# Attention and fp8 layer on one core: both score pairs ahead of the weighing in quads with a fix, side products in two parts

## The reference, cut to what matters

```
h = layernorm(x)                       # no learned scale
q, k, v = h @ Wq, h @ Wk, h @ Wv
latent = (k + v) @ W_down              # 32 wide; k_rec = latent @ W_up_k, v_rec = latent @ W_up_v
scores = clip(q k_rec^T * scale) * decay(|i - j|)
x = x + softmax(clip(scores)) @ v_rec (heads joined) @ Wo
x = x + fp8_gemm(layernorm(x) in bf16, kernel) + bias
```

## Time and profile before

| | |
|---|---|
| median of 3 runs | 525.74 us |
| profiled execution | 525.57 us |
| its span | 523.8 us |
| TensorE, ScalarE, VectorE, GpSimd busy | 93%, 94%, 53%, 42% |
| mean granted TensorE clock | 0.989 |
| first and last exponential start | 14.0, 502.0 us |

### The profile page before, as it was taken

One profiled execution on the slowest core, in us unless ns is written; L12 is line 12 of the kernel. 1 busy time (PEld: TensorE's weight loads), 2 busy tenths in 40 slices (PEclk: granted clock), 3 DMA queues, 4 the chain that ended last, 5 costly groups with the idle time before them and its releaser, 6 DMA issues.

```text
span 523.8 us, 9403 instructions
## 1 busy us (share of the span) xinstructions
PE 486.4 (93%) x3452; PEld 111.6 (21%) x3452; DVE 277.5 (53%) x646; ACT 490.0 (94%) x535; POOL 219.2 (42%) x285
## 2 busy tenths in 40 slices
PE   8899999999999999999999999999999999999961
PEld 3311211122122212122121212122121212121220
DVE  6515554555654564546645564554654564445646
ACT  4789999999999999999999999999999999999961
POOL 0989429790720249971450229992101121002110
PEclk9999999999999999999999999999999999999995
DMA  6689889947994104567966002747977000100000
GB/s 178 200 244 222 312 201 219 335 181 167 248 211 106 29 7 162 203 243 158 256 161 139 8 5 76 272 167 203 262 159 183 8 4 7 48 0 2 1 21 24
DMA packets 50483, 73.79 MB, mean 141 GB/s; under 512 B 6208, under 2 KB 29184, under 8 KB 50432
## 3 DMA queue, kind: packets, MB, share of 16 engines
q1 hardware_dynamic: 49344, 72.72, 50.6%
q10 hardware_dynamic: 1088, 0.41, 0.3%
HBM read 35.40 MB, written 35.65 MB: 136 GB/s over the span
## 4 chain that ended last, share of the span: by engine, by line
PE 56%; ACT 29%; issue 7%; DVE 7%; DVEq 0%; ACTq 0%
ACT probs L770 29%; PE ps L970 27%; PE ps L954 16%; DVE ps L1206 3%; PE ps L834 2%; PE ps L950 2%; PE ps L839 1%; PE ps L867 1%; PE ps L830 1%; PE ps L862 1%; PE ps L809 1%; PE ps L824 0%; PE ps L874 0%; DVE xn L1254 0%; PE ps L880 0%
## 5 line engine op out<-in xcount | busy, mean ns | idle before, releaser
L770 ACT ACTIVATE probs<-ps 128x1024 f32<-128x1024 f32 x512 | 478.9, 1061 | 9.5 <-DVE ps L1206 5.9
L970 PE MATMUL ps<-probs,V 128*9 128x512 f32 x2048 | 267.8, 594 | 3.2 <-ACT probs L770 0.8
L1206 DVE TENSOR_TENSOR ps<-ps,consts 128x256 f32<-128x256 f32 (+1 forms) x256 | 144.3, 566 | 173.3 <-PE ps L954 166.0
L954 PE MATMUL ps<-Qs,Ks 64*128 64x512 bf16 x992 | 179.0, 385 | 13.6 <-ACT probs L770 6.9
L954 PEld LDWEIGHTS ps<-Qs,Ks 64*128 64x128 bf16 x992 | 42.7, 93 | 281.0 <-ACT probs L770 266.5
L970 PEld LDWEIGHTS ps<-probs,V 128*9 128x9 f32 x2048 | 31.3, 88 | 80.5 <-issue 59.8
L572 POOL TENSOR_SCALAR rs<-mv 128x4 f32<-128x4 f32 (+1 forms) x10 | 2.3, 231 | 102.7 <-DVEq L1388 102.2
L1214 DVE COPY pv_out<-ps 105x512 f32<-105x512 f32 x31 | 21.4, 692 | 34.4 <-PE ps L970 34.4
L655 POOL TENSOR_TENSOR xs<-xs,magic 128x512 f32<-128x512 f32 x7 | 8.9, 1278 | 70.3 <-DVE magic L1267 70.3
L606 POOL TENSOR_TENSOR sq<-sq,parts 128x1024 f32<-128x1024 f32 (+1 forms) x16 | 28.4, 1773 | 1.3
L608 POOL TENSOR_TENSOR parts<-sq,parts 128x1024 bf16<-128x1024 f32 (+1 forms) x16 | 28.3, 1771 | 1.3
(11 more groups left out here) (148 smaller groups left out, 280.9 us busy)
## 6 DMA issues: line engine op xcount, KB each, us to landing
Qs<-qp_dram SPq DMA_DIRECT2D x26, 512.0 KB, 8.7
qp_dram<-parts SPq DMA_DIRECT2D x14, 768.0 KB, 5.2
Ks<-kp_dram SPq DMA_DIRECT2D x26, 384.0 KB, 5.7
kp_dram<-parts SPq DMA_DIRECT2D x12, 384.0 KB, 3.4
kp_dram<-parts SPq DMA_DIRECT2D x6, 768.0 KB, 4.4
qp_dram<-parts SPq DMA_DIRECT2D x7, 512.0 KB, 6.3
Qs<-qp_dram SPq DMA_DIRECT2D x10, 256.0 KB, 9.4
X<-L_attn_x SPq DMA_DIRECT2D x9, 256.0 KB, 3.1
```

The costliest lines, as they stand in the source:

```text
L770: nc.scalar.activation(probs[:, quad % RING, 2 * jp:2 * jp + 2, :].rearrange("p j n -> p (j n)"), ps_all[:, bank * CH:(bank + 2) * CH], AC ...
L954: last = nc.tensor.matmul(bank, Ks[half, g, jp, key_cols(v, kc)], Qs[half, g, jp, qh, v, :], start=True, stop=True)
L970: last = nc.tensor.matmul(pv[32 * j:32 * j + VW, :], V[:, unit // 2 * NB + kc, HG * j + g, :], probs[:, quad % RING, j, :], start=i == 0, ...
L1206: nc.vector.tensor_tensor(own, own, factors, ALU.mult).then_inc(fixed, 1)
```

## The change

Four things change. (a) In a quad with a fix (not in the fp32 group) TensorE makes the scores of both slots before it weighs quad - 2, and a side product of that quad lies between the two. (b) The products sp, proj, k, q, v and n (from quad 13 of the program on) are made in two parts, the first two quads ahead of the second; only the second signals, only the first waits. (c) Quads of products move: for batch 1 second keys 28 to 30, first queries 30 to 34; for the later batches first queries 28 to 30 and second queries 38 to 34; the tail's xqT and y of odd units' rows from 30 and 34 to 36 and 38; in the last unit the turns from 12, 18, 26 to 18, 22, 26. (d) VectorE's reciprocals go from quad 7 to quad 6, and GpSimd makes late keys before a result.

```diff
-TAIL_ROWS = [28 if not is_shared(_u) else 34 if _u % 2 else 30 for _u in range(UNITS)]
-TAIL_PRODUCTS = [30 if not is_shared(_u) else 36 if _u % 2 else 34 for _u in range(UNITS)]
+TAIL_ROWS = [(34 if _u % 2 else 36) if is_shared(_u) else 28 for _u in range(UNITS)]
+TAIL_PRODUCTS = [(36 if _u % 2 else 38) if is_shared(_u) else 30 for _u in range(UNITS)]
...
-        (6 if _b else 14, "T", 0), (18, "T", 1), (22 if _b else 26, "k", 0), (26 if _b else 28, "k", 1),
-        (28 if _b else 30, "q", 0), (38, "q", 1), (50, "v", 0), (54, "v", 1))]
+        (6 if _b else 14, "T", 0), (18, "T", 1), (22 if _b else 26, "k", 0), (26 if _b else 30, "k", 1),
+        (30 if _b else 34, "q", 0), (34 if _b else 38, "q", 1), (50, "v", 0), (54, "v", 1))]
...
-JOBS += [((UNITS - 1) * UNIT_QUADS + _q, "turn", _g) for _g, _q in enumerate((12, 18, 26))]
+JOBS += [((UNITS - 1) * UNIT_QUADS + _q, "turn", _g) for _g, _q in enumerate((18, 22, 26))]
...
-PE_SIDE = {_q: (_k, _i) for _q, _k, _i in JOBS}
+PARTED = [_j for _j in JOBS if _j[0] > NB + 4 and _j[1] in ("sp", "proj", "k", "q", "v", "n")]
+PE_SIDE = {_q: (_k, _i, 1 if (_q, _k, _i) in PARTED else None) for _q, _k, _i in JOBS}
+PE_SIDE.update({_q - 2: (_k, _i, 0) for _q, _k, _i in PARTED})
...
                 if b < B - 1:
                     early_parts(b + 1)
+                    late_keys(b + 1)
                     if b > 0:
                         result(2 * b - 1)
-                    late_keys(b + 1)
...
-            def spread_sums(unit, bank):
-                pe.wait_ge(spread, unit + 1)
-                nc.tensor.matmul(bank, same_head, wide[:, :], start=True, stop=True).then_inc(spread_ps, 1)
+            def spread_sums(unit, bank, part=None):
+                if part != 1:
+                    pe.wait_ge(spread, unit + 1)
+                cols = slice(0, CH) if part is None else half_cols[part]
+                last = nc.tensor.matmul(bank[:, cols], same_head, wide[:, cols], start=True, stop=True)
+                if part != 0:
+                    last.then_inc(spread_ps, 1)
...
+            def head_norms(b, bank, part=None):
+                if part != 1:
+                    pe.wait_ge(sq_ready, b + 1)
+                for a in range(2) if part is None else (part,):
...
+                both_first = not in_f32 and variant(quad)[1] is not None
...
                     qk(s)
-                    if quad >= 2 and s % 2 == in_f32:
+                    if s % 2 == 0 and quad in PE_SIDE and both_first:
+                        job(*PE_SIDE[quad])
+                    if quad >= 2 and s % 2 == (in_f32 or both_first):
                         weigh(quad - 2)
-                if quad in PE_SIDE:
+                if quad in PE_SIDE and not both_first:
...
-                if at == 7:
+                if at == 6:
                     invert_sums(unit)
                     widen_sums(unit)
```

More of the change, by code:

```diff
@@ L141 @@
 JOB_ORDER = [(_k, _i) for _, _k, _i in JOBS] + [(_k, UNITS + _n) for _n in range(LOOPED_UNITS) for _k in ("proj", "xqT", "y")]
-PE_SIDE = {_q: (_k, _i) for _q, _k, _i in JOBS}
+PARTED = [_j for _j in JOBS if _j[0] > NB + 4 and _j[1] in ("sp", "proj", "k", "q", "v", "n")]
+PE_SIDE = {_q: (_k, _i, 1 if (_q, _k, _i) in PARTED else None) for _q, _k, _i in JOBS}
+PE_SIDE.update({_q - 2: (_k, _i, 0) for _q, _k, _i in PARTED})
+assert len(PE_SIDE) == len(JOBS) + len(PARTED)
 DVE_SIDE = {_q + (_q > FIRST_VALUES): (_k, _i) for _q, _k, _i in JOBS}
@@ L825, in transpose_x, with columns, own_rows, project_k @@
                 last.then_inc(tr_ps, 1)
[L827 to L837, removed]
+            pairs = (range(0, 2), range(2, 4))
+            def columns(bank, part):
+                return bank if part is None else bank[:, half_cols[part]]
+            def own_rows(n, part):
+                first = n % 2 * CH + (0 if part is None else part * HALF)
+                return slice(first, first + (CH if part is None else HALF))
+            def project_k(n, bank, part=None):
+                if part != 1:
+                    pe.wait_ge(xnT_ready, n + 1)
+                last = nc.tensor.matmul(columns(bank, part), wk_eff[:, :], xnT[:, own_rows(n, part)], start=True, stop=True)
+                if part != 0:
+                    last.then_inc(k_ps, 1)
+            def project_q(n, bank, part=None):
+                last = nc.tensor.matmul(columns(bank, part), wq_s[:, :], xnT[:, own_rows(n, part)], start=True, stop=True)
+                if part != 0:
+                    last.then_inc(q_ps, 1)
+            def project_v(n, bank, part=None):
+                for t in range(4) if part is None else pairs[part]:
                     at = n % 2 * CH + t * P
@@ L840, in project_v @@
                                             start=True, stop=True)
[L841 to L845, removed]
+                if part != 0:
+                    last.then_inc(v_ps, 1)
+            def head_norms(b, bank, part=None):
+                if part != 1:
+                    pe.wait_ge(sq_ready, b + 1)
+                for a in range(2) if part is None else (part,):
                     for half in range(2):
@@ L849, in head_norms @@
                                                 start=True, stop=True)
-                last.then_inc(n_ps, 1)
+                if part != 0:
+                    last.then_inc(n_ps, 1)
             def turn_tops(bank):
@@ L858, in sum_oks, with project_o @@
                 nc.tensor.matmul(bank[0:1, 0:1], oks[:, 0:1], ones[:, :], start=True, stop=True).then_inc(flag_ps, 1)
-            def spread_sums(unit, bank):
-                pe.wait_ge(spread, unit + 1)
-                nc.tensor.matmul(bank, same_head, wide[:, :], start=True, stop=True).then_inc(spread_ps, 1)
-            def project_o(unit, bank):
-                pe.wait_ge(ot_ready, unit + 1)
-                for t in range(4):
+            def spread_sums(unit, bank, part=None):
+                if part != 1:
+                    pe.wait_ge(spread, unit + 1)
+                cols = slice(0, CH) if part is None else half_cols[part]
+                last = nc.tensor.matmul(bank[:, cols], same_head, wide[:, cols], start=True, stop=True)
+                if part != 0:
+                    last.then_inc(spread_ps, 1)
+            def project_o(unit, bank, part=None):
+                if part != 1:
+                    pe.wait_ge(ot_ready, unit + 1)
+                for t in range(4) if part is None else pairs[part]:
                     last = nc.tensor.matmul(bank[:, t * P:(t + 1) * P], OT[:, unit % 2, t * P:(t + 1) * P], wo_s[:, :],
                                             start=True, stop=True)
-                last.then_inc(proj_ps, 1)
+                if part != 0:
+                    last.then_inc(proj_ps, 1)
             def transpose_xq(unit):
@@ L890, in turn_group, with job @@
                 last.then_inc(turn_ps, 1)
-            def job(kind, i):
+            def job(kind, i, part=None):
                 n = JOB_ORDER.index((kind, i))
-                if n > 0:
+                if n > 0 and part != 1:
                     semaphore, value = emptied(*JOB_ORDER[n - 1])
@@ L899, in job @@
                 elif kind == "k":
-                    project_k(i, work)
+                    project_k(i, work, part)
                 elif kind == "q":
-                    project_q(i, work)
+                    project_q(i, work, part)
                 elif kind == "v":
-                    project_v(i, work)
+                    project_v(i, work, part)
                 elif kind == "n":
-                    head_norms(i, work)
+                    head_norms(i, work, part)
                 elif kind == "flags":
@@ L911, in job @@
                 elif kind == "sp":
-                    spread_sums(i, work)
+                    spread_sums(i, work, part)
                 elif kind == "turn":
@@ L916, in job @@
                 elif kind == "proj":
-                    project_o(i, work)
+                    project_o(i, work, part)
                 elif kind == "xqT":
@@ L1009, in _ @@
             weigh(QUADS - 1)
-            pairs = (range(0, 2), range(2, 4))
             for half in range(2):
```

## The result

The changed kernel took 530.94 us (median of 5 runs, 529.24 to 533.0) beside 526.51 for the kernel before (5 runs, 525.65 to 526.9): ratio 1.0087, 95% interval 1.0064 to 1.011. It is slower by 0.9%; 523.6 was forecast, with 526.5 as upper end.

The account below looks back on a forecast made before the run. ScalarE's exponentials were the bound, with 13.5 us of waiting to win. From quad 8 of unit 2, 8.9 - 4.9 - 2.0 = 2.0 us won, so 525.6 - 2.0 = 523.6; range 519.5 to 526.5.

Parts of the forecast that it names:

- What bounds the kernel: ScalarE's exponentials, one every 0.917 us; its 13.5 us kept waiting or late is all a better order can win.
- Step 1: Fixed quads: second score pair no longer waits behind the weighing, so its 0.38 us lateness and the like go.
- Step 2: Side products on TensorE: half pieces cost 0.64 us (0.65 proj and v), each half of the norms 0.98.
- rival B: Halves take 0.53 us, lateness doesn't grow, but 3.8 us of after-stalls go behind the gather: 520.4; chance 0.13.
- step 1's own sum of J - 0.53: Fixed quads: a side product taking J adds J - 0.53 us to the lateness at the next fixed quad.
- Step 3: ScalarE stalls left in units 0 to 7 by TensorE alone: 7.7 us against 13.5, so 5.8 won.
- the two halves of the norms 0.4: Odd units: stall cost of making the norms in two halves, 0.4 us within a unit's 1.7.
- Step 4: Batch 1's keys moved two quads later: late queries +1.3 us, unit 1's last gather lands at 156.0 instead of 154.7.
- Step 5: Unit 2, reciprocals at quad 6: VectorE waits 4.1 us for the gather; fix at 158.0 against 155.96.
- Rival D: Early queries' copy or a later load holds unit 2's gather beyond 159.7; wait 7.8 us, 527.3 to 529; chance 0.12.
- C: GpSimd's chain shifts by up to two quads; gather landing at 158.4 gives 525.9 us; chance 0.16.
- Step 6: Later xqT and y, result behind late keys, later turns: nothing, or 1 us of SP time nobody waits for.

Follow-up runs that it names:

- e10: Kernel of e3 with the old order of a quad, weighing between the two score pairs: 527.55 us, ratio 1.0033 to the kernel before.
- e3: Changed kernel with norms of batch 0 whole and loads of batch 1's third group behind unit 1's last gather: 520.2 us, ratio 0.9888.
- e4: Kernel before with the scores-first order alone, whole side products, nothing moved: 519.8 us, ratio 0.9881.
- e8: Kernel before with the scores-first order and the loads of batch 1's third group behind unit 1's last gather: 518.08 us, ratio 0.9853.
- e6: Changed kernel with all side products whole and the loads of batch 1's third group behind unit 1's last gather: 516.78 us, ratio 0.983.
- e1: Changed kernel with the norms of batch 0 made whole at quad 22 again: 528.28 us, ratio 1.0053 to the kernel before.
- e2: Changed kernel with the loads of batch 1's third group issued behind unit 1's last gather: 523.5 us, ratio 0.9958 to the kernel before.
- e9: Kernel before with only batch 1's second keys moved from quad 28 to 30 and first queries from 30 to 34: 531.97 us, ratio 1.0119.
- e5: Changed kernel with TensorE rewriting one slot's scores 22 times during the wait in unit 2's quad 8: 527.94 us, ratio 1.0042 to the kernel before.

## Why the prediction was wrong

**What bounds the kernel: right.** ScalarE's losses explain the differences of the spans to 0.3 us, but for e10, where the part behind the last exponential is 0.8 us longer too, and every kernel that lost less was faster by about that much: 8.3, 6.0, 4.3 and 3.2 us for 519.8, 518.08, 516.78 and 515.42.

**Step 1, scores first: right.** 5.8 us were forecast for order and pieces together, against 5.4 in e3 (525.6 - 520.2). The order alone gave some 6 in e4 and 7.5 in e8, with the gather's wait out of the way. It is the part of the change that carries.

**Step 2, halves: right in price, wrong in use.** 0.63 and 0.98 came for 0.64 and 0.98, so rival B is out. (Its own sum didn't close: 523.6 less the 3.8 that it names is 519.8, not 520.4. And my four passes of 0.22 are 0.88, not 0.85, which makes a half 0.62.) The Trainium skill (TensorE: Matmul & The Clock Gate, Back-to-back issue gap) lets the gap go with the columns, but for 2.5 ns, an estimated 0.53 for a half of 1.06; the measured 0.63 speaks against using that rule for these products. But my own price should have made me ask whether the pieces pay. Two of them cost 1.26 for 1.06, the norms 1.96 for 1.00. By step 1's own sum of J - 0.53, a whole product adds 0.53 of lateness and the next pair of quads without one takes 0.63 off (3.04 against 3.67); two pieces add 0.11 each and nothing takes it off. The missing row was "order without pieces"; e6 puts it at 3.4 us.

**Step 3, stalls by unit: right** in six units, 6.1 us for 6.0 in units 1 and 3 to 7, and 1.3 for 1.4 in unit 0 once the norms are whole (e1).

**Not in the sum: the input of the norms' first half, 3.9 us.** I priced the piece at quad 20 and didn't look when its squares are ready, though the trace of the kernel before has it (58.4). The prediction counts "the two halves of the norms 0.4" as time of TensorE. Of the 3.9 us 2.2 are the stop and the rest is the slow stretch behind it: in e2, where the same stop was followed by no fall of the clock, these quads lost 2.2. It is not all in the total while the gather is late (e1 won 2.7).

**Step 4, the chain behind the moved keys: the step that failed.** It says that "the DMA wait takes up the rest", that +1.3 us reach the late queries, and that the gather so lands at 156.0. GpSimd and SP in the kernel after:

```profile
81.79 2.63 POOL L599 TENSOR_TENSOR sq<-kT,decay 128x256 f32<-128x256 f32 x2 [23.43 <-DVE kT L1340]
100.85 1.28 POOL L599 TENSOR_TENSOR sq<-kT,decay 128x512 f32<-128x512 f32 x1 [0.18 <-POOL parts L613]
107.87 2.37 POOL L604 TENSOR_TENSOR sq<-qT,decay 128x1024 f32<-128x1024 f32 x1 [1.91 <-DMA qp_dram<-parts]
...
100.75 1.99 SPq L411 DMA_DIRECT2D qp_dram<-parts  x3
116.97 2.00 SPq L411 DMA_DIRECT2D qp_dram<-parts  x3
```

The early keys start 81.79 - 75.21 = 6.6 later. Without the stop at quad 20 they start at 77.45 (e1; I had 78.0), so 2.2 come from the move and 4.3 from the stop. The wait of 2.48 in front of the late keys does vanish (0.18 now). From there on the head's delay is passed on: late queries 107.87 for 102.32, their store 116.97 for 111.42, both 5.5 later, and the gather 161.15 for 154.76, 6.4 later.

Which link of my chain failed, e1 shows. There the late queries start at 103.51, for 103.6 forecast, and their store goes out at 112.60, 1.2 later than before: up to this point the step was right. But the gather landed at 157.90 and not at 156.0. I had let the last leg, from the store through the queue to the landing, pass on just the shift of the store; it came 1.9 us longer, with a DMA share of 1.04 from 145 to 155, where the kernel before had 0.93 and 0.82. So the step failed in two terms: the head was 3.8 us later than I had it (81.79 for 78.0), by the stop, and the last leg was too short, by 0.8 here, 0.9 in e9 and 1.9 in e1. What makes this difference isn't shown, and with one execution each, and 2.8 us between those of after and e5, it may be chance in part.

The 7 us for the store of the early queries were half luck. From issue to the start behind it are 7.1 in after, e1 and e3, but 8.7 in e4 and e9, 8.9 in e2 and e5, and 8.5 in the kernel before itself, where the store goes out at 93.83 and GpSimd starts at 102.32. The trace that I had showed 8.5. SP in the kernel before, and GpSimd in e1:

```profile
93.83 2.62 SPq L406 DMA_DIRECT2D qp_dram<-parts  x3
...
103.51 2.36 POOL L604 TENSOR_TENSOR sq<-qT,decay 128x1024 f32<-128x1024 f32 x1 [1.91 <-DMA qp_dram<-parts]
```

**Step 5, the wait at the reciprocals: the right place, mis-sized.** 5.06 us came for 4.1. What was missing is the clock: I priced a wait by its own length. Behind 4.66 us of TensorE's standing are some 3 us more (e5); behind e1's 5.75 us they are 1.9.

Together, by place: 3.9 (norms), 1.0 (wait), 3.0 (clock) are 7.9 us, and 531.4 of the profiled execution less 523.6 is 7.8. By cause it reads otherwise, since what is lost ahead of unit 2 hides behind the gather: its landing is 5.1 us later than the 156.0 forecast (1.9 in e1, 3.25 more with the stop), which puts the fix of quad 8 at 162.95 for 158.0, and the clock adds 3.0. For e1 the same count gives 523.6 + 1.9 + 1.9 = 527.4, which is what its profiled execution took.

**Rival D.** Its point came true: the gather landed beyond 159.7 and the result was slower than before. I had given it 0.12 and 529 as its worst, because its cause was to be the early queries' copy (which played no part), and because the clock was in no case of mine. A chain in which each store waits for the last, at whose end VectorE already waited 0.43 us, deserved more than that: C and D were one mechanism. Even C's landing was slower than before (e1: 157.90, 528.28), where I had put 525.9 on 158.4; the clock is in neither.

**Step 6: not tested by itself.** Units 3 to 7 of the kernel after lost 4.2 us for 3.9 forecast, so it cost little or nothing there. The 1.3 us from e8 to e6 are of all the moves together.

## What to carry to other kernels

When a product is moved or split, ask of each piece when its input is ready and who waits for its output, not only what it costs on its engine; a chain of store, wait and next store can pass on a delay in full (3.5 us at the head were 4.9 at the end in e9). Price a stop of TensorE above its own length (4.66 us of standing cost 3 us more here, 5.75 us 1.9 more), and put small DMAs that somebody waits for ahead of the bulk loads in their queue.

## What the hardware did that I had not expected

- In stops of 4.66 us (after), 4.41 us (e9) and 5.75 us (e1) the granted clock fell to 0.5 before the stop was over, and stayed there for 6.82 to 6.83 us in all; in e5, with the wait filled by matmuls and 2.21 us of standing left, it stayed at 1.00.
- Stops of about 2.1 us went both ways. In the kernel after, 2.17 us at quad 20 of unit 0 were followed by 3.41 us at half clock, in e5 2.07 us by 3.42; in e2 the same stop was not, as its TensorE shows: the weighing behind takes 1.05.

```profile
58.70 1.05 PE L873 MATMUL ps<-sq,consts 128*32 128x512 f32 x4 [2.09 <-POOL sq L658]
60.00 1.05 PE L1002 MATMUL ps<-probs,V 128*9 128x512 f32 x8
```

  What decides between them these runs don't show. After 1.52 us (e4) there was no fall.
- Halving the norms' matmuls, which run side by side, saves nothing: 0.98 us for half of what takes 1.00. An ordinary fp32 product of half the columns takes 0.63 of 1.06.
- The three DMAs that store the early queries take 7.1 to 8.9 us from issue to the release of who waits for them, and 7.1 and 8.9 in two executions of the same instructions (after, e5), though the profile's own median for such a store, issue to landing, is 4.4 to 6.1 us by its size in the stretch from 86 to 108 of the kernel after.
